# A conditioned transformer layer and a two-way state-space layer on one core: skip term of the forward pass behind the first sum, side steps from half state 8, other states by diagonal

## The reference

```python
# layer 0, for each block
x = x + gt_a * attention(modulated_layernorm(x), Wqkv, Wproj)         # 16 heads, causal
x = x + gt_m * (gelu(modulated_layernorm(x) @ W1 + b1) @ W2 + b2)
# layer 1
def _ssm(h, in_w, xproj_w, dt_bias, A_log, Dskip, out_w):
    xs, z = jnp.split(h @ in_w, 2, axis=-1)                            # 512 channels each
    xs = jax.nn.silu(xs)
    proj = xs @ xproj_w
    dt = jax.nn.softplus(proj[..., :D_INNER] + dt_bias)
    Bm, Cm = proj[..., D_INNER:D_INNER + D_STATE], proj[..., D_INNER + D_STATE:]
    A = -jnp.exp(A_log)
    def step(hst, ins):
        dt_t, B_t, C_t, x_t = ins
        hst = hst * jnp.exp(dt_t[:, :, None] * A) + (dt_t * x_t)[:, :, None] * B_t[:, None, :]
        return (hst, jnp.einsum('bds,bs->bd', hst, C_t))
    ...
    y = ys + xs * Dskip
    return y * jax.nn.silu(z) @ out_w
x = x + gate * (ssm_forward(h) + flip(ssm_backward(flip(h))))
x = x + gate * ((silu(h @ mlp_w1) * (h @ mlp_w2)) @ mlp_w3)
```

## Time and profile before

| | |
|---|---|
| median of 3 runs | 3304.09 us (3300.77 to 3307.41) |
| the profiled execution | 3316.36 us, its span 3314.5 us |
| PE / PEld busy | 92% / 83% of the span |
| DVE / ACT / POOL busy | 87% / 88% / 88% |
| mean granted TensorE clock | 0.97 |

### The profile page before, as it was taken

The page is one execution under the profiler, slowest core; times in us unless marked ns, Lnnn a source line. Parts: engine busy times, 40 slices in busy tenths (PEclk is TensorE's granted clock), DMA queues, the critical chain, the costliest instruction groups (busy, mean ns, idle before and its releaser), DMA issues.

```text
span 3314.5 us, 71769 instructions
## 1 busy us (share of the span) xinstructions
PE 3058.3 (92%) x23032; PEld 2760.6 (83%) x23032; DVE 2884.0 (87%) x3203; ACT 2904.8 (88%) x6357; POOL 2911.3 (88%) x1552
## 2 busy tenths in 40 slices
PE   8778999999999999999999999999999999998877
PEld 6568988898888988889888898888888898887766
DVE  2269999899989998899998999899988999989985
ACT  1189999898989989899998999899898989989993
POOL 0069999998999999999998999999999999999995
PEclk6699999999999999999999999999999999999998
DMA  5011111111111111111111111112111111111210
GB/s 179 0 42 45 45 46 54 43 52 44 46 51 45 52 44 47 51 50 44 46 54 44 51 45 45 53 45 52 44 47 50 51 46 45 45 50 44 55 47 26
DMA packets 163039, 162.61 MB, mean 49 GB/s; under 512 B 17610, under 2 KB 156874, under 8 KB 162644
## 3 DMA queue, kind: packets, MB, share of 16 engines
q1 hardware_dynamic: 162644, 157.69, 17.5%
HBM read 154.44 MB, written 3.18 MB: 48 GB/s over the span
## 4 chain that ended last, share of the span: by engine, by line
PE 50%; ACT 23%; issue 11%; DVE 8%; POOL 7%; DVEq 0%; ACTq 0%; POOLq 0%; DMA 0%; SPq 0%
PE ps L1263 13%; ACT dA L584 12%; PE ps L1247 12%; ACT uBT L570 6%; PE ps L1010 6%; POOL hst L417 5%; DVE hst L909 5%; PE ps L1245 4%; PE ps L1082 3%; PE ps L1019 3%; PE ps L1057 3%; PE ps L1066 1%; PE ps L1255 1%; PE ps L1131 1%; POOL uBT L430 1%
## 5 line engine op out<-in xcount | busy, mean ns | idle before, releaser
L417 POOL TENSOR_TENSOR hst<-hst,C_sb 128x1024 f32<-128x1024 f32 x1024 | 2447.3, 2407 | 176.1 <-DVE hst L909 172.7
L909 DVE TENSOR_TENSOR_SCAN hst<-dA,ps 128x512 f32<-128x512 f32 x2048 | 2376.7, 1203 | 146.3 <-PE ps L1263 112.9
L584 ACT ACTIVATE dA<-dt,A 128x255 f32<-128x255 f32 x4096 | 1745.0, 501 | 1.4 <-DVE hst L909 1.2
L1263 PE MATMUL ps<-ident,hst 128*128 128x128 f32 x8192 | 1240.7, 274 | 46.8 <-POOL hst L417 46.7
L1247 PE MATMUL ps<-ident,uBT 128*128 128x128 f32 x7104 | 1084.5, 275 | 52.6 <-DVE hst L909 39.8
L570 ACT ACTIVATE uBT<-uT,BT 128x512 f32<-128x512 f32 x1376 | 936.4, 717 | 117.3 <-PE ps L1247 89.2
L1263 PEld LDWEIGHTS ps<-ident,hst 128*128 128x128 f32 x8192 | 963.2, 141 | 62.9 <-POOL hst L417 62.2
L1247 PEld LDWEIGHTS ps<-ident,uBT 128*128 128x128 f32 x7104 | 844.6, 142 | 195.3 <-DVE hst L909 69.4
L430 POOL TENSOR_TENSOR uBT<-uT,BT 128x512 f32<-128x512 f32 x400 | 427.2, 1068 | 1.4 <-PE ps L1245 1.4
L1245 PE MATMUL ps<-uBT,uT 128*128 128x128 f32 x2176 | 302.7, 284 | 33.9 <-DVE hst L909 27.9
L1245 PEld LDWEIGHTS ps<-uBT,uT 128*128 128x128 f32 x2176 | 272.9, 197 | 45.7 <-DVE hst L909 35.9
(11 more groups left out here) (146 smaller groups left out, 2176.0 us busy)
## 6 DMA issues: line engine op xcount, KB each, us to landing
C_sb<-c_dram SPq DMA_DIRECT2D x1024, 128.0 KB, 2.9
gate_l<-gate_rows_dram SPq DMA_DIRECT2D x16, 256.0 KB, 3.8
x_att<-in_x_dram SPq DMA_DIRECT2D x8, 256.0 KB, 3.6
w<-in_L_cond_W_dram SPq DMA_DIRECT2D x2, 1024.0 KB
out_dram<-x_glu SPq DMA_DIRECT2D x8, 256.0 KB, 3.1
wg<-in_L_cond_mlp_w_dram SPq DMA_DIRECT2D x3, 512.0 KB, 11.0
w_xp<-_L_cond_fwd_xproj_w_dram SPq DMA_DIRECT2D x1, 1280.0 KB, 12.5
w_xp<-_L_cond_bwd_xproj_w_dram SPq DMA_DIRECT2D x1, 1280.0 KB, 14.4
```

Source lines behind the costliest of these rows:

```text
L417: pool.tensor_tensor(h, h, C_sb[:, n % FED:n % FED + 1, :].to_broadcast([P, KI, NB]), ALU.mult).then_inc(hC_ready.sem, 1)
L584: done = act.activation(dA[:, n % NT, c, lo:hi], dt[:, d, c, lo:hi], ACT.Exp, scale=A[:, d, c, n:n + 1])
L909: dve.tensor_tensor_scan(pair(hst[:, n % NR]), pair(dA[:, n % NT]), ps[:, BANK_U + (2 * n + e) % (2 * NU), :][:, way], 0.0, ALU.mult, ALU. ...
L1263: last = pe.matmul(ps[:, BANK_Y + j, c * P:(c + 1) * P], hst[:, n % NR, c, j * P:(j + 1) * P], ident[:, :], start=False, stop=(n == NS - 1 ...
```

## The change

There are four parts.

1. `BY_DIAGONAL`. In forward passes the states by diagonal were 1, 3, 22 to 27, 61 and 63, and now are 24 to 29, 61 and 63. In backward passes they were 1, 3, 55, 57, 59, 61 and 63, and now are 1, 3, 55, 57 and 59.
2. Forward passes: the first sum of state 0 opens y (it clears each bank), and the skip term is added later, 4 products behind each of two half states: bank 0 behind the second sum of state 0, bank 1 behind the first sum of state 1. Backward passes keep the old order.
3. `FIRST_HALF`: the side steps of forward passes start at half state 8, not 6. The last backward pass keeps its start at 8, the others theirs at 2. Where the last step stands is unchanged, so steps that were moved by 2 half states at first are moved by 1 in the middle and by none from half state 76 on (in the passes of the loop).
4. Nothing else: the number of steps, their order and their contents are the same.

```diff
-    BY_DIAGONAL = ((1, 3, 22, 23, 24, 25, 26, 27, 61, 63), (1, 3, 55, 57, 59, 61, 63))
+    BY_DIAGONAL = ((24, 25, 26, 27, 28, 29, 61, 63), (1, 3, 55, 57, 59))
...
-    FIRST_HALF, LAST_HALF, HEADS_BEFORE = 6, (127, 120), 16
+    FIRST_HALF, LAST_HALF, HEADS_BEFORE = 8, (127, 120), 16
...
-            start = 2 if d == 1 and has_next else FIRST_HALF + 2 * d
+            start = 2 if d == 1 and has_next else FIRST_HALF
...
-            def start_y(p, d):
-
-                pe.wait_ge(g_ready.sem, g_ready.at(p, 0))
-                for j in range(TT):
-                    for c in range(KI):
-                        pe.matmul(ps[:, BANK_Y + j, c * P:(c + 1) * P], xsT[:, c, j * P:(j + 1) * P], skip_diag[:, d, c, :],
-                                  start=(c == 0), stop=False, skip_group_check=True)
-
-            def sum_state(r, n, e):
+            def skip_term(d, j, begins):
+
+                for c in range(KI):
+                    pe.matmul(ps[:, BANK_Y + j, c * P:(c + 1) * P], xsT[:, c, j * P:(j + 1) * P], skip_diag[:, d, c, :],
+                              start=(begins and c == 0), stop=False, skip_group_check=True)
+
+            def sum_state(r, n, e, begins=False):
...
-                                         start=False, stop=(n == NS - 1), is_transpose=True, skip_group_check=True)
+                                         start=(begins and c == 0), stop=(n == NS - 1), is_transpose=True, skip_group_check=True)
...
                     if n == BEHIND and e == 0:
-                        start_y(p, d)
+                        pe.wait_ge(g_ready.sem, g_ready.at(p, 0))
+                        if d == 1:
+                            for j in range(TT):
+                                skip_term(d, j, True)
                     if n >= BEHIND:
-                        sum_state(p * NS + n - BEHIND, n - BEHIND, e)
+                        sum_state(p * NS + n - BEHIND, n - BEHIND, e, d == 0 and n == BEHIND)
                     elif not very_first:
                         sum_state(p * NS + n - BEHIND, NS + n - BEHIND, e)
+                    if d == 0 and (n, e) in ((BEHIND, 1), (BEHIND + 1, 0)):
+                        skip_term(d, 1 - e, False)
```

## The result

The changed kernel took 3333.76 us (median of 6 runs, 3332.17 to 3339.77), the kernel before beside it 3308.19 us (6 runs, 3300.77 to 3310.09): ratio 1.0083, interval 1.0072 to 1.0093 (the ratios here are worked out over all runs, and can differ a little from the ratio of the medians). It is 25.6 us slower. The forecast was 9 us faster, and the result lies above the range.

A forecast was written before the change was run, and what follows sets the result against it. No single bound: TensorE after the gate, ACT around the dts chain. 5 x (-1.9) - 0.7 + 0.5 + 0.7 = -9.0 us on the median of 3304.09 gave 3295.1 us; range 3282 to 3307.

The forecast's parts named there:

- part 4: ACT and L832 at the dts chain: L524 ends 1.1 us earlier, one scan more done behind it; together 2.2 us earlier.
- ACT gains no lead: Rival: ACT's waits at states 4 to 7 only move, L524 comes 0.96 us late; 3305.9 us, chance 0.24.
- Part 1: Start of forward passes, states 1 and 3 without diagonals: gate starts 1.2 us earlier; POOL's 1.5 us a pass costs nothing.
- Part 2: States 4 to 7: state 4's scan could come 2.7 us earlier, but TensorE bounds, leaving only the gate's 1.2.
- the first rival: Behind the gate TensorE bounds less closely than read, so the 2.7 us stay gained; 3283.1 us, chance 0.18.
- part 3: States 12 to 23: TensorE's savings, less one product more, bring DVE to state 23 2.8 us earlier, 3.3 at most.
- Part 5: States 28 and 29 by diagonal: 1.8 us more TensorE work, mostly covered by its waits for scans; 0.3 us lost.
- the lead is carried to the end: From half state 76 on steps stand where they stood, so each of five passes keeps its gain of 1.9 us.
- The clock rival: TensorE's longer wait at the gate brings a stretch at its lower clock level; 3312.1 us, chance 0.12.
- the clock under transposes alone: Rival: from backward passes' last steps to half state 8, transposes alone let TensorE's clock fall; 3357 us, chance 0.02.
- The last item of the list: Last sign of being wrong: passes lose after half state 46 what they had won; no size given.

The follow-up runs named there:

- psum_input: Changed kernel, but in forward passes 2 to 14 L832 reads its first input from PSUM, leaving out softplus's correction term: 3315.43 us, ratio 1.0021.
- ends_only: Kernel before, with states 1 and 3 of forward and 61 and 63 of backward passes no longer by diagonal: 3312.27 us, ratio 1.0013.
- diag_24_29: Kernel before, with states 24 to 29 by diagonal in place of 22 to 27 in forward passes: 3315.81 us, ratio 1.0026.
- start8_only: Kernel before, with only the side steps of forward passes starting at half state 8: 3322.69 us, ratio 1.0042.
- before_again: Kernel before, unchanged, run once more for a second profile: 3303.93 us (one run), span 3302.1 us.
- split_start8: Changed kernel with the diagonals of before, keeping the split skip term and the start at half state 8: 3319.35 us, ratio 1.0039.
- chain_back: Changed kernel, with forward passes' side steps from dts step 17 on at the half states of the kernel before: 3316.02 us, ratio 1.0023.

## Why the prediction was wrong, point by point

**The step that failed is part 4**, "Behind it one scan more is done (1.1 us). Together **2.2 us earlier** once the chain is through". It priced the move of L832 as a gain and didn't ask what POOL does at that instant. It took the 2.35 us of L832's row as fixed, and half of them was a wait. The row was there to be read: 2.35 us for 128x1024, where L895 of the earlier trace rows took 1.22 for the same size. L832 took 4.80 us in four of six passes. Taking only L832's hold away (psum_input) gives back 14.6 us of traced time. Instead of 2.2 us earlier in each of the passes the chain came out 2.1 us later on average (12.8 us in six). Next, L524 ended 73.1 us behind the first scan in pass 4, before 73.2 (means of passes 4 to 12: 73.0, and 73.1 and 72.4 in the two profiles of before): ACT had a lead of 0.1 us or none, not 1.1. L832 was to wait 1 us or more for it, and waited 0.1 us at most. The rival "ACT gains no lead" was right on that and mis-sized the rest.

**Part 1** failed: the gate did not come 1.2 us earlier. Over passes 4 to 12 it starts 10.07 us behind the first scan on average, before 10.67 and 9.93. The saving on TensorE is real (0.87 for 1.65 us), but TensorE resumes later behind the branch, 1.8 us behind the first scan on average instead of 1.0 and 0.9. Why the first force waits there longer isn't settled. POOL's 1.5 us a pass, costed at nothing, does not show in ends_only between state 4 and the end.

**Part 2** was right in mechanism: the scan of state 4 at once, the half states at 1.74 us, the lead given back. So the first rival, that the whole stall comes back, did not come true. By state 22 all of it was gone, -15.9 + 18.7 us, where part 3 counts on 0.7 us a pass. (Its own terms leave 1.2 - 0.7 = 0.5, and in part 4 2.0 - 0.96 is 1.04, not 1.1. Both slips are small beside the miss.)

**Part 3** failed: no lead of 2.8 us at state 23. Between states 10 and 22 the change lost 0.3 us a pass. diag_24_29 shows what became of the 1.8 us of states 22 and 23: the scan came 0.4 us earlier, and L524, which L832 waits for, not at all. ACT, not TensorE, sets that stretch.

**Part 5** was mis-sized, and with the debt of the steps it makes the 12.0 us behind state 28: 1.0 us a pass for diagonals at 28 and 29 (diag_24_29), not 0.3. And "the lead is carried to the end" missed the debt. The steps stood where they stood from half state 76 on, so the one that was put off was paid for before that, 0.9 us a pass in states 30 to 38 of start8_only and 1.2 in all behind state 28.

**The other passes.** Pass 14 was to gain nothing and lost 3.4 us against before_again (2.0 against the profile shown); the four operations held DVE there for 11.95 us instead of 9.84, L832 for 5.94. Pass 0 was to lose 0.5 us and won 1.1; ends_only by itself lost 0.6. Pass 15 was to lose 0.7: from its first scan to its last it lost 0.6, as said, and the 1.7 us that came back behind the last scan are a stretch that differs between kernels and executions (43.9 us here, 45.6 and 45.8 in the two profiles of before, 44.9 in start8_only). In the last pass POOL is busy 170.00 of 170.00 us, as said:

```profile
3116.20:3286.20 170.00, 127.54 (x1040) 114.03 (x1040) 144.61 (x127) 149.74 (x319) 170.00 (x92) 1.00 0.18 48
```

**The clock rival** was seen in part. Weight loads and the stretch behind the gate of pass 10 of the changed kernel:

```profile
2148.28 0.42 PEld L1261 LDWEIGHTS ps<-ident,hst 128*128 128x128 f32 x4 [2.14 <-POOL hst L417]
```

```profile
2148.90:2152.30 3.40, 3.40 (x18) 3.40 (x17) 2.72 (x3) 2.88 (x7) 3.40 (x3) 0.50 0.24 67
```

TensorE had waited 2.14 us, and the granted clock then is 0.50 (the lower level, 1.2 GHz) for 3.4 us. The same stretch of pass 12 reads 0.50 too (2541.40 to 2544.80). In passes 10 and 12 states 4 to 10 took 1.6 us more than in the others, 3.3 us together. In pass 4, behind a wait of 1.90 us, it stayed at 1.00. At the gates of passes 2 and 14 there is no fall now, where pass 2 had one before. The rival of the clock under transposes alone did not come true: from 2911.00 to 2931.20, at the end of pass 13 and the start of pass 14, TensorE has nothing but transposes, and the granted clock is 1.00.

**The last item of the list**, passes that lose after half state 46 what they had won, is what happened, and it was named as what nothing foresaw. A range that had taken the hold of DVE by POOL into account, from 2.35 against 1.19 us, would have had a case on the slow side; it had none but the clock.

## What to carry to other kernels

Where a duration in a row is twice that of a neighbour of the same shape, look at what other engines do in that stretch before the instruction is moved: the difference is a wait that the profile counts as busy, and it goes by the new place. An operation of DVE with two inputs in SBUF is best put where POOL is about to run dry; with POOL at 88% there are few such places, and one half state decided over 2 us a pass. And steps that are put off at the start and must be done by the same place are paid for in the next stretch that their engine bounds.

## What the hardware showed

- DVE's operations with two inputs in SBUF (L832, L835, L839, L843) and POOL's L417, L427 and L430 were never seen to run at full pace side by side. L832 took 1.23 us alone and up to 4.83 beside POOL in the loop (up to 6.20 in pass 14, in split_start8); in return POOL's L427 took 1.62 instead of 0.63, L417 3.26 to 3.36 instead of 2.37 and L430 2.1 instead of 1.07. With one input in PSUM the same operation took 1.23 us beside a busy POOL.
- Which one waits differs. In passes 2, 6, 8 and 12 L832 waited through two whole instructions of POOL and the rest of a third, and got through when POOL went idle; in passes 4 and 10 it came in between two. The code is the same in all of them, and L832 starts 0.80 to 0.84 us ahead of the end of POOL's L417 in all six. In chain_back it gets its turn at the next boundary where it started 0.80 us ahead, and waits on where it started 0.82 ahead; in the kernel before, 0.68 against 0.69 to 0.71. So a few hundredths of a us go with the outcome; what decides it isn't shown.

The Trainium skill states the rule in "SBUF — State Buffer", section "Who interferes with whom": the port pair that VectorE and GpSimd share is an exclusive lock, a VectorE instruction with two SBUF inputs contends with a GpSimd instruction that reads SBUF, and one with at most one SBUF input (outside the 2-port modes) does not. The Trainium skill adds on the same page, in "Summary: rules for kernel authors", that the second one to issue blocks until the first finishes; read strictly, L832 would wait for one L417 at most, which is an estimate of 2.4 us from that rule and L417's time in the trace. The trace agrees on the lock (1.23 us alone, 4.80 beside POOL) and on PSUM inputs (1.23 us beside a busy POOL), and differs on the bound: L832 waited 3.6 us, across two boundaries between instructions of POOL.
